# New orders of work, a shorter step of the median search, shorter gates, one norm on VectorE and no drain at the end, in a one-core conv-gate and mixture-of-experts kernel

## What is computed

```python
a = _ln_c(x)                                    # norm over channels
mean, mx, std = a.mean(-1), a.max(-1), a.std(-1, ddof=1)   # for each batch, channel
u = stack([mean, mx, std], -1)
med = median(u.reshape(b, -1), -1)              # of 1536 values of each batch
u = (u - med) ** 3
z = einsum('bck,ck->bc', u, cfc_w) / sqrt(1 + 1e-5) * bn_w + bn_b
x = x + a * sigmoid(z)[:, :, None, None]

t = tokens(x)                                   # 2048 x 512
n = _ln_t(t)                                    # norm over channels
logits = n @ router_w.T                         # 8 experts, the best one is taken
glu = lambda x, wg, wu, wd: silu(x @ wg) * (x @ wu) @ wd
t = t + sigmoid(best logit) * glu(n, expert's weights) + glu(n, shared weights)
```

## Time and profile before

| | us |
|---|---|
| median of 3 runs | 441.52 |
| lowest, highest | 441.19, 442.17 |
| profiled execution | 440.67 |
| its span, first to last instruction | 438.7 |
| TensorE busy (share) | 401.7 (92%) |
| VectorE busy | 239.6 (55%) |
| ScalarE busy | 192.6 (44%) |
| GpSimd busy | 191.1 (44%) |
| chain that ended last: TensorE, VectorE, GpSimd, issue | 71%, 7%, 6%, 5% |
| mean granted TensorE clock | 0.976 |

### The profile page before, as it was taken

How to read it: one execution, slowest core, us unless ns; L and a number is a source line. 1 busy time by engine, 2 the same in 40 slices (tenths; PEclk the granted TensorE clock), 3 DMA queues, 4 the chain that set the end, 5 groups by cost and what they waited for, 6 DMA issues and landing times.

```text
span 438.7 us, 7610 instructions
## 1 busy us (share of the span) xinstructions
PE 401.7 (92%) x2006; PEld 312.9 (71%) x2007; DVE 239.6 (55%) x540; ACT 192.6 (44%) x319; POOL 191.1 (44%) x263
## 2 busy tenths in 40 slices
PE   7877779899999998999999799999999999999981
PEld 3534468687778877888887587887778788777860
DVE  6879454787345443434697257365275736474330
ACT  4986256765772444542103344153264324361120
POOL 5996623554333453586021972416224440514110
PEclk9969699999999999999999999999999999999996
DMA  8900101011111361114344468537556754723100
GB/s 282 387 6 0 48 24 50 1 48 50 48 49 49 131 277 48 49 48 145 120 141 124 150 213 326 201 106 256 188 192 222 250 200 145 251 84 120 44 35 16
DMA packets 15885, 56.23 MB, mean 128 GB/s; under 512 B 2607, under 2 KB 2607, under 8 KB 12400
## 3 DMA queue, kind: packets, MB, share of 16 engines
q1 hardware_dynamic: 10976, 40.93, 25.6%
q0 software_dynamic: 4880, 14.95, 10.3%
HBM read 43.28 MB, written 13.63 MB: 130 GB/s over the span
## 4 chain that ended last, share of the span: by engine, by line
PE 71%; DVE 7%; POOL 6%; issue 5%; ACT 5%; DMA 3%; DVEq 1%; SPq 0%; POOLq 0%; ACTq 0%
PE GU L1539 39%; PE YHX L1539 20%; PE YHX L1531 3%; PE YHX L1524 3%; PE YHX L1569 2%; ACT w_raw L709 2%; DMA x_sb<-x_tok 1%; POOL roots L437 1%; DMA tiles<-xn_d,tokidx 1%; ACT hT L756 1%; DVE xT L1093 1%; PE A L1425 1%; DVE hT L1107 1%; POOL w_parts L463 1%; POOL tok_rstd L430 1%
## 5 line engine op out<-in xcount | busy, mean ns | idle before, releaser
L1539 PE MATMUL GU<-w_parts,xT 128*128 (+1 forms) x864 | 215.5, 398 | 5.0 <-issue 4.6
L1539 PEld LDWEIGHTS GU<-w_parts,xT 128*128 128x128 f32 x864 | 158.7, 189 | 40.9 <-issue 10.4
L1539 PE MATMUL YHX<-w_parts,hT 128*128 (+1 forms) x432 | 108.1, 399 | 1.7 <-DVE hT L1107 1.7
L1539 PEld LDWEIGHTS YHX<-w_parts,hT 128*128 128x128 f32 x432 | 78.6, 188 | 18.3 <-issue 2.8
L580 POOL DMA_INDIRECT out<-x_sb,scatidx x20 | 27.7, 1387 | 106.1 <-DVE x_sb L1372 99.6
L756 ACT ACTIVATE hT<-YHX 128x512 fp32r<-128x512 f32 x36 | 21.5, 597 | 107.0 <-PE YHX L1531 107.0
L1107 DVE TENSOR_TENSOR hT<-YHX,hT 128x512 fp32r<-128x512 f32 x36 | 24.8, 690 | 65.0 <-ACT hT L756 61.2
L1113 DVE TENSOR_TENSOR hidden<-hidden,GU 128x512 f32<-128x512 f32 x36 | 24.7, 686 | 52.0 <-issue 43.3
L746 ACT ACTIVATE xT<-YHX 128x512 fp32r<-128x512 f32 x37 | 22.1, 598 | 63.7 <-PE YHX L1524 63.4
L1367 DVE TENSOR_TENSOR w_parts<-w_raw,w_parts 128x2048 f32 x19 | 43.5, 2289 | 5.0 <-ACT w_parts L855 3.0
L855 ACT ACTIVATE w_parts<-w_raw 128x2048 f32 (+1 forms) x21 | 39.4, 1911 | 0.0
(11 more groups left out here) (240 smaller groups left out, 453.2 us busy)
## 6 DMA issues: line engine op xcount, KB each, us to landing
w_raw<-weights SPq DMA_DIRECT2D x27, 1024.0 KB, 5.6
xn_d<-tiles SPq DMA_DIRECT2D x16, 256.0 KB, 2.0
z_d<-x_sb SPq DMA_DIRECT2D x16, 256.0 KB, 2.3
x_sb<-x_tok SPq DMA_DIRECT2D x7, 512.0 KB, 8.2
x_sb<-x_tok SPq DMA_DIRECT2D x2, 256.0 KB, 2.7
tiles<-xn_d,tokidx POOLq DMA_INDIRECT x21, 4.4
x_sb<-z_d,tokidx POOLq DMA_INDIRECT x20, 5.2
out<-x_sb,scatidx POOLq DMA_INDIRECT x20
```

Source lines behind the costliest of these rows:

```text
L1539: last = pe.matmul(dst, left[:, lp, kc, :], wset(q, k, wp, kc), start=(i == 0), stop=(i == 3 * KC - 1))
```

## The change

1. **Load and first statistics.** Tile 2 is loaded by a DMA of its own, and its statistics are taken when it has landed. For batch 0 VectorE adds the epsilon and negates the mean, and GpSimd only takes the root. constants() runs before token_stats(0); tile_start, rev8 and the offsets of groups of two are made later.
2. **Orders in the head.** VectorE: half of token_stats(3) before channel_stats(1), channel_stats(2) before channel_maxima(1), the repetitions of batches 3 and 4 before x_lo(1). GpSimd: token_rstd(3) before the weights' low parts, rstd_tile(0) right behind first_lo(DOWN, 2), ahead of channel_std(3). TensorE: other numbers of filler matmuls, up_product(0) right behind the first half of the values, route(0) before the second half.
3. **Search.** Thresholds lie at other distances. `ahead` is now thr plus a difference, made behind the comparison; a step ends with one operation, and low is only made by the last.
4. **Median and gates.** The batch norm's factor is multiplied into the convolution's weights once; the gates are (u w)(u u) with one operation fewer, the medians too.
5. **Tile 0.** VectorE adds the epsilon, GpSimd takes the root, VectorE normalises tile 0 into tiles, between the two halves of first_gated(1); ScalarE's norm_x(0) goes.
6. **Iterations.** In iterations whose BEGIN holds a search step, VectorE moves thr before h_lo. In iterations 0 to 2 ScalarE runs its MIDDLE count before the silu. token_stats of batches 6 and 7 and their token_rstd move to the end of the iteration before. In iteration 8, tile 10 is turned before up_product(9) and routed before down_product(8).
7. **Table.** shares() moves from in front of gated(15) to behind x_lo(16), block_experts() to right behind gated(15), slot_shares() to the end, fill_slots(1) behind transpose_x(17). The table's memory moves (tab to gate_rows, its scratch to a_tiles).
8. **End.** `nc.Block(no_gpsimd_drain=True)`.

The diff, cut to its core:

```diff
+DISTANCES = {3: (17 / 16, 51 / 2 ** 11, 19 / 2 ** 15, 57 / 2 ** 22, 85 / 2 ** 28),
+             2: (45 / 64, 89 / 2 ** 13, 11 / 2 ** 16, 11 / 2 ** 22, 11 / 2 ** 28)}
...
-        block = ctx.enter_context(nc.Block())
+        block = ctx.enter_context(nc.Block(no_gpsimd_drain=True))
...
+        def first_bank_of(b):
+            return 4 if b == 2 else 2 * b + 1
+        def maxima_of(b):
+            return 5 if b == 1 else 2 * (b + 1)
+        def turned_in(n):
+            tiles_of = TURNED_AT.get(n, ())
+            return tiles_of if len(tiles_of) == 2 else (None, *tiles_of)
...
# SP
+            for h in range(2):
+                sp.dma_start(x_sb[:, 2 + h, :], xt[2 + h]).then_inc(x2_in if h == 0 else x_in[1], 16)
...
# GpSimd: token_rstd, rstd_tile, orders
+                if b == 0:
+                    own(pool.tensor_tensor(r, r, powers[:, 0, 0:2], ALU.pow))
+                    pool.tensor_tensor(m, m, r, ALU.mult).then_inc(rstd_a, 1)
+                    return
...
+                if t == 0:
+                    pool.tensor_tensor(r, r, powers[:, 0, 0:1], ALU.pow).then_inc(rstd_b, 1)
+                    return
...
-            first_lo(GATE, 0)
             token_rstd(3)
-            for part in range(1, QUARTERS):
+            for part in range(QUARTERS):
                 first_lo(GATE, part)
...
             first_lo(DOWN, 2)
-            first_lo(DOWN, 3)
+            rstd_tile(0)
             channel_std(3)
             repeat_std(3)
-            rstd_tile(0)
             rstd_tile(1)
+            first_lo(DOWN, 3)
...
+                if n + 1 in STATS_AT:
+                    token_rstd(STATS_AT[n + 1])
...
# ScalarE, iterations
                 h_hi(n)
+                if n in STATS_AT:
+                    before(n, MIDDLE)
                 silu_gate(n + 1, (n + 1) % 2)
                 after(n, BEGIN)
-                before(n, MIDDLE)
+                if n not in STATS_AT:
+                    before(n, MIDDLE)
...
# VectorE: search
-                if i + 1 < SEARCH_STEPS:
-                    note(dve.tensor_scalar(ahead[0:n], steps[size][0:n, i + 1:i + 2], low[0:n], None, ALU.add))
...
+                note(dve.tensor_tensor(ahead[0:n], thr[0:n], steps[size][0:n, i + 1:i + 2], ALU.add))
...
                     dve.scalar_tensor_tensor(out=thr[0:n], in0=mb[0:n, 0:1], scalar=group_step(g, i), in1=ahead[0:n],
                                              op0=ALU.mult, op1=ALU.add).then_inc(thr_ready, 1)
-                dve.scalar_tensor_tensor(out=low[0:n], in0=mb[0:n, 0:1], scalar=group_step(g, i), in1=low[0:n],
-                                         op0=ALU.mult, op1=ALU.add).then_inc(row_used, 1)
-                dve.wait_ge(row_used, rows_read(g, i) + 1)
+                    dve.wait_ge(thr_ready, counts_before(g, i) + 2)
+                else:
+                    dve.scalar_tensor_tensor(out=low[0:n], ..., in1=ahead[0:n], ...).then_inc(row_used, 1)
...
# VectorE: gates
-                own(dve.tensor_tensor(cube, u, u, ALU.mult))
-                own(dve.tensor_tensor(cube, cube, u, ALU.mult))
-                own(dve.tensor_tensor(cube3, cube3, cw, ALU.mult))
+                note(dve.tensor_tensor(cube, u, u, ALU.mult))
+                own(dve.tensor_tensor(u3, u3, cw, ALU.mult))
+                own(dve.tensor_tensor(cube, cube, u, ALU.mult))
                 own(dve.tensor_reduce(zs, cube.rearrange("p (b k s) -> p b k s", b=size, s=3), AX_X, ALU.add))
-                own(dve.scalar_tensor_tensor(out=zs, in0=zs, scalar=-1.0 / (1.0 + BN_EPS) ** 0.5, in1=bnw, op0=ALU.mult, op1=ALU.mult))
...
# VectorE: tile 0
+            def first_norm_x():
+                dve.wait_ge(rstd_b, 1)
+                dve.tensor_scalar(tiles[:, 0, :], x_sb[:, 0, :], x1_mv[:, 0, 0:1], x1_rstd[:, 0:1],
+                                  ALU.subtract, ALU.mult).then_inc(first_xn, 1)
...
# TensorE: head and iterations
             spread_values(1, 0)
+            up_product(0, x_slot(0), 0, 0)
             pe.wait_ge(router_ready, 1)
-            up_product(0, x_slot(0), 0, 0)
+            route(0)
             spread_values(1, 1)
-            route(0)
             route(1)
...
                 transpose_h(n, n % 2)
+                early, *turned = turned_in(n)
+                if early is not None:
+                    turn_x(early)
                 up_product(n + 1, x_slot(n + 1), 0, 0)
...
# VectorE: table
             slot_places()
-            shares()
             gated(n + 3, 1)
+            block_experts()
             add_shared(n + 2)
             h_lo(n + 3)
             x_lo(n + 4, block_slot(0))
-            slot_shares()
-            block_experts()
+            shares()
+            block_table()
             add_shared(n + 3)
-            block_table()
             x_lo(n + 5, block_slot(1))
             gated(n + 4, 0)
+            slot_shares()
```

More of the change, by code:

```diff
@@ L355, in _ @@
                 sp.dma_start(x_sb[:, h, :], xt[h]).then_inc(x0_in if h == 0 else x_in[0], 16)
-            for b in range(1, 5):
+            for h in range(2):
+                sp.dma_start(x_sb[:, 2 + h, :], xt[2 + h]).then_inc(x2_in if h == 0 else x_in[1], 16)
+            for b in range(2, 5):
                 load_x(b)
@@ L970, in start_search @@
                 size = len(GROUPS[g])
-                own(dve.memset(low, SEARCH_FROM))
                 dve.tensor_scalar(thr, steps[size][:, 0:1], SEARCH_FROM, None, ALU.add).then_inc(thr_ready, 1)
@@ L1124, in _ @@
             channel_maxima(0)
+            token_half(3, 0)
             channel_stats(1)
+            channel_stats(2)
             channel_maxima(1)
-            channel_stats(2)
             channel_maxima(2)
@@ L1130, in _ @@
             start_search(0)
-            token_stats(3)
+            token_stats(3, (1,))
             for i in range(SEARCH_STEPS):
@@ L1138, in _ @@
             token_stats(4)
+            scale_weights()
             medians(0)
@@ L1181, in _ @@
             for n in range(NT - 4):
-                if n:
-                    before(n, BEGIN)
+                if n == 0:
+                    token_stats(STATS_AT[0])
+                before(n, BEGIN)
                 if n - 1 in STATS_AT:
                     channel_stats(STATS_AT[n - 1])
-                if n in STATS_AT:
-                    token_stats(STATS_AT[n])
-                if n == 0:
-                    before(n, BEGIN)
+                searching = any(what in ("count", "spread") for what, _, _ in VISITS.get((n, BEGIN), ()))
+                if searching:
+                    after(n, BEGIN)
                 h_lo(n)
-                after(n, BEGIN)
+                if not searching:
+                    after(n, BEGIN)
                 if n - 1 in STATS_AT:
@@ L1195, in _ @@
                 before(n, MIDDLE)
+                early, *turned = turned_in(n)
+                if early is not None:
+                    x_lo(early, x_slot(early))
                 gated(n + 1, (n + 1) % 2)
-                for t in TURNED_AT.get(n, ()):
+                for t in turned:
                     x_lo(t, x_slot(t))
@@ L1201, in _ @@
                     measure_x1(t)
+                if early is not None:
+                    keep_logits(early)
+                if n + 1 in STATS_AT:
+                    token_half(STATS_AT[n + 1], 0)
                 add_shared(n)
+                if n + 1 in STATS_AT:
+                    token_stats(STATS_AT[n + 1], (1,))
                 before(n, END)
-                for t in TURNED_AT.get(n, ()):
+                for t in turned:
                     keep_logits(t)
@@ L1658, in _ @@
                 transpose_h(n, n % 2)
+                early, *turned = turned_in(n)
+                if early is not None:
+                    turn_x(early)
                 up_product(n + 1, x_slot(n + 1), 0, 0)
-                for t in TURNED_AT.get(n, ()):
+                for t in turned:
                     turn_x(t)
                 visit(n, MIDDLE)
+                if early is not None:
+                    route(early)
                 down_product(n, 0, 0)
@@ L1722, in _ @@
             transpose_x(n + 5, xg[:, 1, :])
+            pe.wait_ge(slots_ready, 2)
+            fill_slots(1)
             up_product(n + 4, block_slot(0), 1, 3)
```

139 lines of the change are left out of this document (87 added, 52 removed).

## The result

The changed kernel takes 426.5 us (median of 4 runs, 425.94 to 428.95) against 441.44 for the kernel before: a ratio of 0.967, 95% interval 0.964 to 0.971. The profiled execution took 426.06 us, with a span of 424.1, which is 14.6 us less than the span before. Single stages differ from the forecast by more than that total shows. Of the executions of all runs, one (of `table_old`, 498.77 us at a mean clock of 0.75) was slow and is left out.

A forecast was written before the change was run, and what follows sets the result against it. TensorE was taken as the fixed bound from 245 to 420 us, with time available in head, iterations, table and end: 5.6 + 5.0 + 1.5 + 5.1 = 17.2; 440.67 - 17.2 + 0.85 = 424.3 us, range 420 to 430.5.

The forecast's parts named there:

- The likeliest case: Whole kernel: the forecast of 424.3 us with its bounds, 421.5 to 427, drain gone; chance 0.53.
- the search: Group 0's search in the head ends 1.6 us earlier, 0.45 of it from count following thr sooner.
- the table: Table stage: reordering finishes the table near 240.0 us, register reading staying serial behind it; 1.5 us, bounds 0 and 2.5.
- the move of the norm: Head: VectorE normalises tile 0, GpSimd runs only the root; x_lo(0) 3.2 us earlier, 1.9 of them from before.
- the first product: TensorE's first product in the head takes 4.5 us, between 3.0 at full clock and 5.9 at half; 0.35 lost.
- rival 2: VectorE and GpSimd collide at the norm and tile 1's combining, x_lo(0) 1.4 us later: 425.7 us; chance 0.10.
- Behind it: After the first product: repeated statistics made during it and logit reading hidden remove TensorE's waits, 2.75 us.
- Iterations: TensorE's waits for counts, iteration 8's transposition, statistics and logits mostly go: 5.0 us, bounds 3.5 and 5.7.
- The end: End of block: GpSimd's drain goes without its work reappearing, 5.1 us gained.
- Rival 1: End: the drain's time moves outside the block instead of vanishing, 429.4 us; chance 0.27.
- Rival 3: Iterations and table: new orders pass waits on, only half of 6.5 us gained, 427.5 us; chance 0.08.
- Rival 4: Clock stays at half into the iterations; two whole iterations would give 444 us, slower than before; chance 0.02.

The follow-up runs named there:

- table_old: Changed kernel with the table stage's old order (shares before gated(15), fill_slots(1) ahead again) : 428.31 us, ratio 0.971.
- old_search_step: Changed kernel with the old search step (low kept, ahead made from low before the next count): 423.55 us, ratio 0.960.
- norm_on_scalar: Changed kernel with tile 0's second norm back on ScalarE, its shift on GpSimd behind the root: 426.98 us, ratio 0.968.
- old_fillers: Changed kernel with the earlier kernel's numbers of filler products on TensorE in the head: 426.34 us, ratio 0.966.
- the pointer: Changed kernel with ahead made by a tensor_scalar taking thr as pointer instead of two SBUF tensors: 423.92 us, ratio 0.961.
- drain_kept: Changed kernel with nc.Block() as before, so the GpSimd drain stays: 432.41 us, ratio 0.981.
- changed_again: The changed kernel unaltered, measured again as base for later runs: 425.95 us, ratio 0.967.

## Why the prediction was right, and which steps were not

The forecast was 424.3 us, the result 426.5: inside the range, 2.2 above. The likeliest case came true (the drain gone, no lasting loss of clock), but the sum of 17.2 us has become 14.6 between the two profiled executions. Two steps failed, the search and the table, and of a third gain one part, the move of the norm, brought nothing. That the total stayed close is partly luck: the first product ran at its lower bound and gave back half of what the search lost.

**The search failed.** The step "now ahead is made while TensorE sums, so the count can follow thr by about 0.2" is right by its row (0.19), and the cost of what was moved was missed: `ahead` had become an instruction with two SBUF tensors, beside ten pieces of GpSimd. Instead of 0.45 us gained on three steps, each step costs 0.16 more than before, the first `ahead` takes 1.20 us and the last operation of the search, low_diag, 0.93 (0.39 in the kernel before, 0.33 in `old_search_step`). Moving token_rstd(3) ahead brought first_norm(6) forward as predicted (22.32), but it could not bring the search forward. At z that is 3.06 us between forecast and trace: 1.06 had arisen at the second comparison, 1.03 in the next three steps, 0.39 behind the last comparison, where the kernel before makes no `ahead`, and 0.54 in low_diag. The row for the rule stood in the earlier trace rows (1.41 beside GpSimd; the same combining takes 0.69 in the changed kernel with GpSimd idle); rival 2 used it, at the wrong place. It expected the collision at the norm and at the combining of tile 1, where nothing happened: 0.55 and 0.68 us, with the root of channel_std(3) on GpSimd from 44.91 to 45.93.

**The norm of tile 0.** The size was right: 1.3 us forecast, 1.61 measured from z to x_lo(0). Of what the prediction bundled here, the move to VectorE was not needed: `norm_on_scalar` gets 2.1 without it. What brought the gain is on GpSimd's side: nothing stands ahead of the root, and the combining of tile 0 meets no piece of GpSimd (0.69 against 1.41, near the 0.6 forecast for that row).

**The first product** was put at 4.5 us "in the middle"; it took 2.99, the lower bound. The fillers did it (`old_fillers`: 4.30). That gave back 1.5 of the 3.06. The head came out at 4.4 us instead of 5.6.

**Behind it** 2.75 forecast, 2.85 measured.

**Iterations**: 5.0 forecast, 4.6 measured. Iteration 8 brought 2.45 (14.05 to 11.6), more than the 2.0 taken. Iteration 1 brought 0.4 (13.97 to 13.59), not the 1.7 of its waits. A part of it is the same fault again. Rows of VectorE, GpSimd and TensorE in the changed kernel:

```profile
76.56 0.86 DVE L997 COPY w_raw<-stats 128x168 f32<-128x168 f32 x2
...
77.41 1.18 DVE L1041 TENSOR_TENSOR search<-search,steps 128x1 f32<-128x1 f32 x1
```

```profile
77.24 1.33 POOL L521 TENSOR_TENSOR x_sb<-x_sb,tiles 128x512 f32<-128x512 f32 x1
```

```profile
77.54 0.18 PE L1558 MATMUL mb<-fewer,same 128*128 128x1 bf16 x1 [1.18 <-DVE fewer L1040]
83.09 0.18 PE L1558 MATMUL mb<-fewer,same 128*128 128x1 bf16 x1 [0.75 <-DVE fewer L1040]
```

`ahead` ends with GpSimd's pass (78.59 and 78.57), and gated and x_lo stand behind it. With the pointer the second wait falls from 0.75 to 0.16 and the iteration to 13.06, so `ahead` accounts for 0.5 of the 1.3 us that are missing. The first wait stays (1.23). Ahead of that comparison stand VectorE's copies (L997), 0.86 us across two passes of GpSimd where the kernel before took 0.40; no run tests them.

**Table stage**: 1.5 forecast, 0.6 left. At TensorE 2.4 were gained at the table and 1.5 lost in the first block, and 0.3 more among the blocks. The failed sentence is "The register reading is serial behind the table": TensorE's products ran on without a gap, while VectorE's reading, which before fell under TensorE's wait (VectorE idle for 5.94 us ahead of h_lo at 248.73), is no longer hidden by it. That the last wait of one engine covers the same work on another was the omitted part.

**The end**: 5.1 forecast, 5.1 measured between the last block's transposition and the end of the span, 1.96 us outside it as before. Rival 1 is refuted by the time outside the span, and `drain_kept` confirms the price. For rival 1 the prediction had named the Trainium skill (Runtime: NRT & Kernel Launch, The ~15us preamble/postamble breakdown); these runs show no wait of the drain's length behind the kernel instead (1.96 us without it, 2.08 with it in `drain_kept`).

Rival 3 was partly true: at the table the wait was passed on, by 1.5 us; in the iterations it was not. Rival 4 did not come: the clock is 1.00 from 58 to 202 us and from 234 to 410 us.

## What to carry to other kernels

A tiny operation on VectorE that reads two SBUF tensors can wait until a pass of GpSimd ends (up to 1.20 of 1.23 us here); written with a pointer operand it did not, so in a serial loop beside GpSimd count SBUF inputs before counting operations. Look at copies and casts as well: they too took up to 1.30 us instead of 0.31. Fillers that hold the clock have an end of their own: when the chain in front of them gets shorter, look whether the product behind them starts with no wait, and try fewer. When an order removes one engine's wait, list what the other engines did under it, and what the third engine does under those.

## What was not expected of the hardware

- One addition of a single element per partition took 1.20, 0.69, 0.70 and 0.15 us, depending on where in GpSimd's pass of 1.23 us it fell, or on there being none; a loop that contains it locks to GpSimd's beat (steps of 2.44 to 2.46 us in the changed kernel, 2.44 and 2.45 in `changed_again`).
- Not every GpSimd instruction held VectorE up: combining with two SBUF inputs took 0.68 us beside a root on GpSimd of 1.02 us. Which do is left open. It goes the other way too: in `norm_on_scalar` GpSimd's shift of one element took 0.73 us beside VectorE's combining, 0.27 elsewhere.
- An operation with a single SBUF input was held up as well when it was a cast or a copy: the cast of the router's weights took 1.30 us in `norm_on_scalar`, 0.31 in the changed kernel and 0.17 in the kernel before, where GpSimd's passes had ended.
- The same 16 filler products took 3.61, 4.47, 4.57 and 5.84 us in executions whose instructions ahead of them were equal or nearly so, as the stretch of half clock in the head falls elsewhere each time (between 25 and 40 us); what places it is open. That moved x_lo(0) by 0.7 us in executions with an identical head, as much as some of the edits were worth.
- A wait of 2.95 us on TensorE left the clock full in the kernel before, one of 2.43 us in `table_old` was followed by a product at half clock (4.60 us). What differs ahead of the two was not studied.
